# Keys one slot ahead, and the products with the values two slots at a time

## The chip, the cores and the metric

The program runs on one core of a Trainium2 chip. The number that counts is the time of one execution in device microseconds (us), the median of several runs. The core has five engines that work side by side and tell each other of finished work through semaphores: TensorE (PE in the rows: matrix products), VectorE (DVE), ScalarE (ACT), GpSimd (POOL) and the queue that issues the transfers (SP). Each engine takes its own instructions strictly in their order; one that waits holds up all behind it on that engine.

## The reference, cut to what matters

A decoder layer over 32 sequences ("batches") of 112 tokens with 512 features: self-attention, cross-attention to 375 context tokens, a quantised feed-forward layer, each with residuals and layer norms. Only the cross-attention is touched:

```python
q = proj(hs, Wq, bq, S)          # 16 heads of 32
k = proj(at, Wk, bk, T)          # T = 375
v = proj(at, Wv, bv, T)
scores = jnp.einsum('bhsd,bhtd->bhst', q, k) / scale
scores = jnp.clip(scores, -50.0, 50.0)
...
probs = jax.nn.softmax(scores, axis=-1)
ctx = jnp.einsum('bhst,bhtd->bhsd', probs, v)
...
delta = _nan_clean(ctx @ Wo.T + bo)
...
delta = (delta - mu) / jnp.sqrt(var + EPS_LN) * ln_gamma + ln_beta
```

## The kernel before

Three stages follow each other, with a barrier between: `self_attention`, `cross_attention`, `ffn`. In `cross_attention` each batch is worked in four slots h = 0 to 3; a slot holds 4 of the 16 heads. The order on each engine is written out by hand in the `body` functions, and `steps` runs batches 0 and 1, a loop of pairs, and batches 30 and 31.

The work of one batch on TensorE, all products in float32 or as three products of split halves (`PASSES`):
- `keys(b, m)`: 12 matmuls of 376 columns (L874) give the keys of slot m in a bank of PSUM, `bKV`; ScalarE adds the bias and moves them into `kf[:, m, :]` (L730).
- `values(b, t)`: 12 matmuls of 512 columns (L887) for one third t of the context tokens; ScalarE moves them into `v` (L736).
- scores (L942): 24 recorded matmuls that use 32 rows of the array each, four at a time, into the four banks of `bSC`. ScalarE takes the exponentials into `pr[h % 2]` (L751), VectorE clamps and masks them in three pieces (L841), GpSimd adds the three pieces into `psum` (L701, L704).
- `attend(b, h)`: the products of the exponentials with the values (L919), 24 recorded matmuls that use 32 columns of the array each, and `sums(b, h)`: 8 more in the same layout that sum the exponentials over the tokens (L928), both into bank `bPV[h % 2]`.
- VectorE divides (`attended`: L787, L789, L793, L795) and writes the split halves `cT`.
- `output(b)`: 12 matmuls of 512 columns with the output weights (L900). VectorE's `tail1` (L800 to L808), `tail2` (L813 to L825) and `tail3` (L829, L831) finish the batch, with a power on GpSimd between them (`norm` L690, `norm2` L694).

The context of a batch comes in by a transfer into `craw`; ScalarE (`split_high`, L723) and VectorE (`split_low`, L767) split it into `cx`.

What order holds before: in slot h of batch b, TensorE makes scores(b, h), then `attend` and `sums` of the slot before, then in slot 1 `output(b - 1)`, and then the keys of slot h of the NEXT batch and one of its thirds of values. So before the first scores all four slots of keys and all three thirds of values of batch 0 are made, and in batch 31 no keys or values are left. `pr` has two buffers.

## Time and profile before

| | |
|---|---|
| median of 3 runs | 1554.0 us (1553.78 to 1556.58) |
| the profiled execution | 1554.15 us, of which its span (first to last instruction) 1552.3 us |
| self-attention and its set-up | from 0 to about 395 us |
| cross-attention, first matmul | at 400.3 us |
| cross-attention, scores of batch 1 slot 0 / batch 31 slot 0 | at 443.5 us / 1257.9 us |
| feed-forward, first instruction | at 1300.3 us |
| TensorE busy over the span | 94% |
| VectorE, ScalarE, GpSimd busy | 70%, 41%, 37% |
| mean granted TensorE clock, share of full | 0.975 |

In the rows, times are from the start of the span. A matmul's own duration includes time in which the next one already runs; so what a block of matmuls costs is read from its start to the start of the next block. "L874" is line 874 of the kernel before; the new kernel has other line numbers for the same code.

### The profile page before, as it was taken

What the parts mean: (1) busy time and instruction counts of PE and PEld (TensorE: products, weight loads), DVE (VectorE), ACT (ScalarE), POOL (GpSimd) and SP (SyncE); (2) the same over time, 40 slices, a digit from 0 to 9 for tenths busy, and PEclk for the clock granted to TensorE, in tenths of its full rate; (3) what the DMA queues carried; (4) which work ended last, traced back from release to release, by engine and by line L of the source; (5) the groups of instructions that cost most, each with busy time, mean ns of one, the idle gap of its engine ahead of it and who ended that gap; (6) DMA issues with size and microseconds to landing.
All of it is one profiled execution on the core that took longest, in us unless ns stands there. A gap on an engine that the chain in (4) does not pass through costs nothing. (4 is left out here: it accounts for less than half of the span.)

```text
span 1552.3 us, 33463 instructions
## 1 busy us (share of the span) xinstructions
PE 1457.4 (94%) x13281; PEld 1129.5 (73%) x13290; DVE 1080.9 (70%) x2039; ACT 640.8 (41%) x828; POOL 567.0 (37%) x487
## 2 busy tenths in 40 slices
PE   7999999997899999999999999999999974998886
PEld 3688888886788888888888888888888852554332
DVE  3756665653278787777778777777877785775788
ACT  2333333332343333434343343434333322888852
POOL 0000000000045455544545554454555453651453
PEclk9999999998899999999999999999999986999999
DMA  6022222322411112121211212121121103287953
GB/s 210 28 83 92 98 98 98 99 102 63 133 34 59 56 38 75 38 75 38 60 53 38 75 38 75 38 61 52 39 74 38 56 13 92 70 284 268 342 183 109
DMA packets 80405, 138.58 MB, mean 89 GB/s; under 512 B 4882, under 2 KB 52498, under 8 KB 78562
## 3 DMA queue, kind: packets, MB, share of 16 engines
q1 hardware_dynamic: 80354, 137.87, 27.5%
q8 instruction: 35, 0.57, 0.2%
q14 instruction: 16, 0.13, 0.0%
HBM read 93.82 MB, written 44.04 MB: 89 GB/s over the span
## 5 line engine op out<-in xcount | busy, mean ns | idle before, releaser
L874 PE MATMUL xa_bKV<-xa_cx,wA 128*128 128x376 f32 x1536 | 289.6, 338 | 7.4 <-DVE xa_cx L767 7.4
L887 PE MATMUL xa_bKV<-wZ,xa_cx 128*125 128x512 f32 x1152 | 288.7, 399 | 0.0
L874 PEld LDWEIGHTS xa_bKV<-xa_cx,wA 128*128 128x128 f32 x1536 | 266.9, 189 | 22.1 <-issue 13.1
L841 DVE TENSOR_SCALAR xa_pr<-xa_pr,xa_keep 125x448 f32<-125x448 f32 x384 | 151.8, 452 | 162.5 <-ACT xa_pr L751 162.2
L701 POOL TENSOR_TENSOR xa_psum<-xa_pr 125x448 f32<-125x448 f32 x128 | 148.0, 1157 | 296.1 <-DVE xa_pr L841 296.1
L887 PEld LDWEIGHTS xa_bKV<-wZ,xa_cx 128*125 128x125 f32 x1152 | 208.7, 186 | 54.6 <-issue 10.6
L730 ACT ACTIVATE xa_kf<-xa_bKV,xa_bk 128x376 f32<-128x376 f32 x128 | 73.5, 575 | 293.4 <-PE xa_bKV L874 293.3
L751 ACT ACTIVATE xa_pr<-xa_bSC 125x1344 f32<-125x1344 f32 x128 | 165.6, 1293 | 40.4 <-PE xa_bSC L942 40.4
L704 POOL TENSOR_TENSOR xa_psum<-xa_psum,xa_pr 125x448 f32<-125x448 f32 x128 | 149.9, 1171 | 12.3 <-POOL xa_psum L701 4.4
L736 ACT COPY xa_v<-xa_bKV 125x512 f32<-125x512 f32 x96 | 56.3, 587 | 205.8 <-PE xa_bKV L887 205.8
L1311 PE MATMUL ff_bF<-w2q,ff_hq 128*128 128x512 bf16 x439 | 102.7, 392 | 24.0 <-DVE ff_hq L1228 22.1
L942 PEld LDWEIGHTS xa_bSC<-xa_qf,xa_kf 32*125 32x125 f32 x3072 | 95.3, 183 | 36.2 <-issue 36.2
L942 PE MATMUL xa_bSC<-xa_qf,xa_kf 32*125 32x112 f32 x3072 | 118.0, 282 | 1.2 <-ACT xa_pr L751 1.2
L787 DVE RECIPROCAL xa_rinv<-xa_bPV 128x112 f32<-128x112 f32 x128 | 109.0, 851 | 0.0
L795 DVE SCALAR_TENSOR_TENSOR xa_cT<-xa_at,xa_bv,xa_cT 128x112 fp32r<-128x112 f32 x128 | 103.3, 807 | 4.6
L919 PE MATMUL xa_bPV<-xa_pr,xa_v 125*32 125x112 f32 x3072 | 101.3, 265 | 5.2 <-DVE xa_pr L841 4.9
L1311 PEld LDWEIGHTS ff_bF<-w2q,ff_hq 128*128 128x128 bf16 x448 | 44.4, 101 | 82.0 <-issue 32.0
L900 PE MATMUL xa_bKV<-wQ,xa_cT 128*112 128x512 f32 x384 | 99.7, 409 | 3.4 <-DVE xa_cT L795 3.4
L1289 PE MATMUL ff_bF<-ff_xqT,w1q 128*128 128x448 bf16 x512 | 99.3, 355 | 0.5 <-DVE ff_xqT L1198 0.5
L227 POOL TENSOR_TENSOR sa_rstd<-sa_ve,sa_half 112x4 f32<-112x4 f32 x8 | 8.1, 1007 | 235.4 <-DVE sa_ve L356 235.4
L472 PE MATMUL sa_bM<-wZ,sa_xn 128*112 128x512 f32 x384 | 90.7, 395 | 0.0
L694 POOL TENSOR_TENSOR xa_rstd<-xa_ve,xa_half 112x1 f32<-112x1 f32 x32 | 59.7, 1865 | 74.4 <-DVE xa_ve L825 74.4
(170 smaller groups left out, 2208.4 us busy)
## 6 DMA issues: line engine op xcount, KB each, us to landing
wraw<-in_ctxT SPq DMA_DIRECT2D x32, 752.0 KB, 5.5
ff_hr<-h_scratch SPq DMA_DIRECT2D x7, 2048.0 KB, 11.1
wraw<-in_w SPq DMA_DIRECT2D x8, 1024.0 KB, 7.6
sa_raw<-in_x SPq DMA_DIRECT2D x8, 896.0 KB, 5.8
x_scratch<-sa_qraw SPq DMA_DIRECT2D x8, 896.0 KB, 5.0
xa_qf<-q_scratch SPq DMA_DIRECT2D x32, 224.0 KB, 5.4
xa_x<-x_scratch SPq DMA_DIRECT2D x32, 224.0 KB, 5.0
x_scratch<-xa_x SPq DMA_DIRECT2D x32, 224.0 KB, 2.3
```

Source lines behind the costliest of these rows:

```text
L701: nc.gpsimd.tensor_tensor(psum01[:], third(h, 0), third(h, 1), ALU.add).then_inc(p01_ok, 1)
L704: nc.gpsimd.tensor_tensor(psum[h % 2][:], psum01[:], third(h, 2), ALU.add).then_inc(ps_ok, 1)
L751: nc.scalar.activation(pr[h % 2][:], bSC[0:TW, :, 0:TC * S], ACT.Exp, scale=XSCALE).then_inc(exp_ok, 1)
L787: nc.vector.reciprocal(rinv[:], bank[:, S:2 * S]).then_inc(ri_ok, 1)
L795: nc.vector.scalar_tensor_tensor(out=cT[1][:, h, :], in0=at[:], scalar=bvt[:, h:h + 1], in1=cT[0][:, h, :].bitcast(F32), op0=ALU.add, op1= ...
L841: nc.vector.tensor_scalar(third(h, t), third(h, t), EM50, bound, ALU.max, ALU.min).then_inc(pr_ok, 1)
L874: mm = nc.tensor.matmul(bKV[par][:, 0:TP], w["k"][l][:, c, m * P:(m + 1) * P], cx[par][r][:, c, :], start=c == 0 and k == 0, stop=c == C - ...
L887: mm = nc.tensor.matmul(bKV[1 - par][0:TW, 0:D], cx[par][l][:, c, t * TW:(t + 1) * TW], w["v"][r][:, c, :], start=c == 0 and k == 0, stop= ...
L900: mm = nc.tensor.matmul(bKV[1 - par][0:S, 0:D], cT[l][:, c, :], w["o"][r][:, c, :], start=c == 0 and k == 0, stop=c == C - 1 and k == 2)
L919: mm = nc.tensor.matmul(bank[j * HD:(j + 1) * HD, 0:S], v[par][:, t, h * P + j * HD:h * P + (j + 1) * HD], pr[h % 2][:, j, t * S:(t + 1) * ...
L942: mm = nc.tensor.matmul(bSC[0:TW, j, t * S:(t + 1) * S], kf[own, h, t * TW:(t + 1) * TW], qf[par][own, h, :], start=True, stop=True)
L1311: mm = nc.tensor.matmul(bF[(UT * u + j) % 8][:, 0:D], hq[:, u % 2, k * M2 + m, j * P:(j + 1) * P], w2q[:, k * M2 + m, :], start=k == 0 and ...
```

## The change

Four things are changed, all in `cross_attention`:
- Keys are made one slot ahead instead of four: slot h makes the keys of slot h + 1 of the same batch, and slot 3 those of slot 0 of the next. Values: slot 0 makes third 2 of its own batch, slots 2 and 3 make thirds 0 and 1 of the next. `output(b - 1)` stays in slot 1, now without values beside it. Each slot now has one block of keys and one block of 512-column matmuls.
- `attend` and `sums` are made two slots at a time: in slot 2 those of slots 0 and 1, in slot 0 of the next batch those of slots 2 and 3. VectorE's `attended` follows in pairs; `pr` has four buffers.
- Keys always use bank `bKV[0]`, values and output `bKV[1]`.
- On VectorE, `split_low` moves from slot 2 to the head of slot 1 (one batch later), `tail2` from slot 2 to the head of slot 3, ahead of that slot's clamps; on GpSimd `norm2` moves ahead of the sums of slot 3; on ScalarE `split_high` moves from slot 1 to slot 3.

```diff
-        pr = [n.sb(f"pr{i}", [TW, NJ, TC * S]) for i in range(2)]
+        pr = [n.sb(f"pr{i}", [TW, NJ, TC * S]) for i in range(C)]
...
             def body(b, par, pair):
                 for h in range(C):
-
+                    if h == 3 and not first(b):
+                        norm2(b - 1)
                     pool.wait_ge(pr_ok, 12 * b + 3 * h + 3)
...
-            for h in range(C):
-                keys(0, 0, h)
-                if h < TC:
-                    values(0, 0, h)
-                if h == 1:
-                    split_high(1, 1)
+            values(0, 0, 0)
+            keys(0, 0)
+            values(0, 0, 1)
+            split_high(1, 1)
...
-                    wait(act, pv_done, s - 1)
-                    wait(act, ps_ok, s - 1)
-                    nc.scalar.activation(pr[h % 2][:], bSC[0:TW, :, 0:TC * S], ACT.Exp, scale=XSCALE).then_inc(exp_ok, 1)
...
+                    wait(act, pv_done, s - 3)
+                    wait(act, ps_ok, s - 3)
+                    nc.scalar.activation(pr[h][:], bSC[0:TW, :, 0:TC * S], ACT.Exp, scale=XSCALE).then_inc(exp_ok, 1)
+                    if h == 3 and not (isinstance(b, int) and b >= B - 2):
                         split_high(b + 2, par)
+                    if h < C - 1:
+                        keys(b, h + 1)
+                    elif not last(b):
+                        keys(b + 1, 0)
+                    if h == 0:
+                        values(b, par, 2)
+                    elif h >= 2 and not last(b):
+                        values(b + 1, 1 - par, h - 2)
...
             def body(b, par, pair):
                 for h in range(C):
+                    if h == 1 and not last(b):
+                        split_low(b + 1, 1 - par)
+                    if h == 3 and not first(b):
+                        tail2(b - 1, 1 - par)
                     dve.wait_ge(exp_ok, 4 * b + h + 1)
...
-                    if h > 0:
-                        attended(b, h - 1)
-                    elif not first(b):
+                    if h == 0 and not first(b):
+                        attended(b - 1, C - 2)
                         attended(b - 1, C - 1)
...
+                    if h == 2:
+                        attended(b, 0)
+                        attended(b, 1)
...
-                    if h > 0:
-                        attend(b, par, h - 1)
-                        sums(b, h - 1)
-                    elif not first(b):
-                        attend(b - 1, 1 - par, C - 1)
-                        sums(b - 1, C - 1)
-                    if h == 1 and not first(b):
-                        output(b - 1, 1 - par)
-                    if not last(b):
-                        if h >= 2:
-                            values(b + 1, 1 - par, h - 1)
-                        keys(b + 1, 1 - par, h)
-                        if h == 0:
-                            values(b + 1, 1 - par, 0)
+                    if h == 2:
+                        for i in range(2):
+                            attend(b, par, i)
+                            sums(b, i)
+                    elif h == 0 and not first(b):
+                        for i in range(2, C):
+                            attend(b - 1, 1 - par, i)
+                            sums(b - 1, i)
+                    if h < C - 1:
+                        keys(b, par, h + 1)
+                    elif not last(b):
+                        keys(b + 1, 1 - par, 0)
+                    if h == 0:
+                        values(b, par, 2)
+                    elif h == 1:
+                        if not first(b):
+                            output(b - 1)
+                    elif not last(b):
+                        values(b + 1, 1 - par, h - 2)
```

TensorE before the change, in the middle of the loop, slots 3 and 0 of a batch; each row is a first matmul with the semaphores it waits for, or the 11 (or 3) after it:

```order
L942 MATMUL xa_bSC<-xa_qf,xa_kf 125x112 x11
L915 ISA
L919 MATMUL xa_bPV<-xa_pr,xa_v 32x112 [waits xa_cthi_ok,xa_pr_ok]
L919 MATMUL xa_bPV<-xa_pr,xa_v 32x112 x11
L928 MATMUL xa_bPV<-xa_psum,xa_ones 32x112 [waits xa_ps_ok]
L928 MATMUL xa_bPV<-xa_psum,xa_ones 32x112 x3
L882 REGISTER_ALU
L887 MATMUL xa_bKV<-wZ,xa_cx 125x512 [waits xa_v_ok]
L887 MATMUL xa_bKV<-wZ,xa_cx 125x512 x11
```

TensorE after the change, in the middle of the loop, slot 0 and into slot 1:

```order
L906 MATMUL xa_bPV<-xa_pr,xa_v 32x112 [waits xa_cthi_ok,xa_pr_ok]
L906 MATMUL xa_bPV<-xa_pr,xa_v 32x112 x11
L915 MATMUL xa_bPV<-xa_psum,xa_ones 32x112 [waits xa_ps_ok]
L915 MATMUL xa_bPV<-xa_psum,xa_ones 32x112 x3
L902 ISA
L906 MATMUL xa_bPV<-xa_pr,xa_v 32x112 [waits xa_cthi_ok,xa_pr_ok]
L906 MATMUL xa_bPV<-xa_pr,xa_v 32x112 x11
...
L915 MATMUL xa_bPV<-xa_psum,xa_ones 32x112 x3
L867 MATMUL xa_bKV<-xa_cx,wA 128x376 [waits xa_k_ok]
...
L929 MATMUL xa_bSC<-xa_qf,xa_kf 125x112 x11
L867 MATMUL xa_bKV<-xa_cx,wA 128x376 [waits xa_k_ok]
```

The blocks of 32-column matmuls now stand in pairs, and in every second slot the keys follow the scores at once.

VectorE after the change, around slot 3 (the names carry their buffer numbers: `bPV0` and `bPV1` belong to the two slots of a pair, `pr3` to slot 3):

```order
L842 TENSOR_SCALAR xa_pr2<-xa_pr2,xa_keep 125x4x112 x3
L786 RECIPROCAL xa_rinv<-xa_bPV0 128x112
...
L786 RECIPROCAL xa_rinv<-xa_bPV1 128x112
...
L794 SCALAR_TENSOR_TENSOR xa_cT1<-xa_at,xa_bv,xa_cT0 128x112
L812 TENSOR_TENSOR xa_rr<-xa_rstd,xa_rs 112x1
L816 SCALAR_TENSOR_TENSOR xa_x11<-xa_dl,xa_rr,xa_x11 112x512
L819 BN_STATS xa_st<-xa_x11 112x6
L822 BN_AGGR xa_mv<-xa_st 112x2
L824 TENSOR_SCALAR xa_ve2<-xa_mv 112x1
...
L842 TENSOR_SCALAR xa_pr3<-xa_pr3,xa_keep 125x4x112 x3
```

The same place before (the clamps of slot 3 write `pr1`):

```order
L825 TENSOR_SCALAR xa_ve2<-xa_mv 112x1
...
L767 TENSOR_TENSOR xa_cx01<-wraw,xa_cx00 128x1504
...
L841 TENSOR_SCALAR xa_pr1<-xa_pr1,xa_keep 125x4x112 x3
L787 RECIPROCAL xa_rinv<-xa_bPV0 128x112
L789 TENSOR_TENSOR xa_at<-xa_bPV0,xa_rinv 128x112
```

Before slot 3's clamps VectorE now has two `attended` and `tail2` in a row, where it had one `attended`, `tail2` and `split_low`.

## Rows read from the trace of the kernel before

**Rows 1.** Windows: busy time by engine, then granted clock, DMA share, GB/s.

```profile
395.50:405.70 10.20, 5.40 (x16) 5.14 (x17) 3.54 (x7) 2.02 (x2) 0.16 (x2) 0.50 0.70 166
443.50:1257.90 814.40, 814.40 (x9604) 681.08 (x9604) 626.25 (x1229) 312.80 (x359) 405.21 (x330) 1.00 0.17 51
1272.70:1289.80 17.10, 8.52 (x75) 5.68 (x76) 11.77 (x22) 0.00 (x0) 6.74 (x7) 0.50 0.23 67
```

**Rows 2.** Timeline, TensorE, loop: start, busy, line, out<-in, rows*columns, count.

```profile
816.77 0.92 PE L942 MATMUL xa_bSC<-xa_qf,xa_kf 32*125 32x112 f32 x24
817.63 0.78 PE L919 MATMUL xa_bPV<-xa_pr,xa_v 125*32 125x112 f32 x24
...
818.53 3.02 PE L887 MATMUL xa_bKV<-wZ,xa_cx 128*125 128x512 f32 x12
...
825.29 2.34 PE L874 MATMUL xa_bKV<-xa_cx,wA 128*128 128x376 f32 x12
827.47 2.94 PE L887 MATMUL xa_bKV<-wZ,xa_cx 128*125 128x512 f32 x12
830.33 0.92 PE L942 MATMUL xa_bSC<-xa_qf,xa_kf 32*125 32x112 f32 x24
```

**Rows 3.** The same, windows of one nanosecond: later matmuls of the small blocks.

```profile
817.75 0.37 PE L919 MATMUL xa_bPV<-xa_pr,xa_v 125*32 125x112 f32 x8
818.13 0.28 PE L919 MATMUL xa_bPV<-xa_pr,xa_v 125*32 125x112 f32 x4
818.32 0.28 PE L928 MATMUL xa_bPV<-xa_psum,xa_ones 125*32 125x112 f32 x4
```

**Rows 4.** Timeline, TensorE, from the first matmul to batch 1, slot 0.

```profile
400.30 4.10 PE L874 MATMUL xa_bKV<-xa_cx,wA 128*128 128x376 f32 x12 [7.43 <-DVE xa_cx L767]
...
407.67 2.23 PE L874 MATMUL xa_bKV<-xa_cx,wA 128*128 128x376 f32 x12
409.74 2.94 PE L887 MATMUL xa_bKV<-wZ,xa_cx 128*125 128x512 f32 x12
...
419.47 0.92 PE L942 MATMUL xa_bSC<-xa_qf,xa_kf 32*125 32x112 f32 x24
420.32 2.34 PE L874 MATMUL xa_bKV<-xa_cx,wA 128*128 128x376 f32 x12
...
443.48 0.92 PE L942 MATMUL xa_bSC<-xa_qf,xa_kf 32*125 32x112 f32 x24
```

**Rows 5.** Timeline, TensorE, batch 31: scores of slot 0, and output(31).

```profile
1257.88 0.92 PE L942 MATMUL xa_bSC<-xa_qf,xa_kf 32*125 32x112 f32 x24
...
1285.14 5.14 PE L900 MATMUL xa_bKV<-wQ,xa_cT 128*112 128x512 f32 x12 [3.42 <-DVE xa_cT L795]
```

**Rows 6.** Timeline, VectorE, the same batch as Rows 2.

```profile
809.50 0.68 DVE L800 TENSOR_TENSOR xa_dl<-xa_bKV,xa_bo 112x512 f32<-112x512 f32 x1
...
811.42 0.74 DVE L808 SCALAR_TENSOR_TENSOR xa_dl<-xa_dl,xa_mv,xa_gam 112x512 f32<-112x512 f32 x1
...
816.93 0.15 DVE L813 TENSOR_TENSOR xa_rr<-xa_rstd,xa_rs 112x1 f32<-112x1 f32 x1
...
819.07 1.73 DVE L767 TENSOR_TENSOR xa_cx<-wraw,xa_cx 128x1504 fp32r<-128x1504 f32 x1
820.71 1.17 DVE L841 TENSOR_SCALAR xa_pr<-xa_pr,xa_keep 125x448 f32<-125x448 f32 x3
...
824.38 0.53 DVE L829 TENSOR_SCALAR xa_x<-xa_x,xa_mv,xa_rstd 112x512 f32<-112x512 f32 x1
```

**Rows 7.** Timeline, GpSimd, the same batch: the power of norm2, the second sum.

```profile
819.21 2.00 POOL L694 TENSOR_TENSOR xa_rstd<-xa_ve,xa_half 112x1 f32<-112x1 f32 x1 [2.33 <-DVE xa_ve L825]
...
823.19 1.14 POOL L704 TENSOR_TENSOR xa_psum<-xa_psum,xa_pr 125x448 f32<-125x448 f32 x1
```

**Rows 8.** Timeline, ScalarE, the same batch: keys moved, exponentials taken.

```profile
816.88 0.57 ACT L730 ACTIVATE xa_kf<-xa_bKV,xa_bk 128x376 f32<-128x376 f32 x1 [1.47 <-PE xa_bKV L874]
817.76 1.29 ACT L751 ACTIVATE xa_pr<-xa_bSC 125x1344 f32<-125x1344 f32 x1 [0.31 <-PE xa_bSC L942]
```

More of the change, by code:

```diff
@@ L708, in body @@
                         norm(b - 1)
-                    if h == 2 and not first(b):
-                        norm2(b - 1)
             steps(pool, body, B, 2)
@@ L904, in _ @@
             pe.wait_ge(const_ok, 2)
-            for h in range(C):
-                keys(0, 0, h)
-                if h < TC:
-                    values(0, 0, h)
+            values(0, 0, 0)
+            keys(0, 0, 0)
+            values(0, 0, 1)
             def attend(b, par, h):
```

69 lines of the change are left out of this document (24 added, 45 removed).

## The prediction

> **What bounds the kernel now.** First the windows: from 443.50 to 1257.90 us TensorE is busy in all of the 814.40 us, at the full granted clock of 1.00 (2.4 GHz) [rows 1]. No wait ends last in this stage; TensorE's own order of work does. So an edit there is worth what it takes out of TensorE's blocks, start to start, as long as nothing else comes late. One batch takes (1257.88 - 443.48) / 30 = 27.147 us [rows 4, 5].
>
> Next the timeline of one batch. From start to start, scores cost 0.86 us (816.77 to 817.63), attend and sums together 0.90 (817.63 to 818.53), keys 2.18 (825.29 to 827.47) and a 512-column block 2.86 (827.47 to 830.33): 6.80 per slot, 27.2 per batch [rows 2]. The small blocks run in groups of four matmuls. Attend's second group starts at 817.75 and its last at 818.13, four groups later: a pitch of 0.095. But the first group takes 0.12 (817.63 to 817.75), 0.025 more; and from the last group of sums (818.32) to the next full-array block (818.53) it is 0.21, 0.115 more than a pitch [rows 2, 3]. So each stay in the 32-column layout costs 0.14 us beside its work. Where scores are followed by keys with no attend between (only batch 0, slot 0), they cost 0.85, just as before attend [rows 2, 4]: leaving the scores costs the same whatever comes next.
>
> Last, the two ends. The first scores start 19.17 us after the first matmul (400.30 to 419.47) [rows 4], after four blocks of keys and three of values; and in batch 31, without keys and values, TensorE waits much of the time (at the end it is busy 8.52 of 17.10 us [rows 1]): its last output starts 27.26 us after the scores of slot 0 (1257.88 to 1285.14) [rows 5].
>
> **TensorE in the loop: less.** The matmuls are the same. Four stays in the 32-column layout per batch become two, so 2 x 0.14 = 0.28 us less per batch: 26.87. The new slots: an even one is scores 0.86, a pair (8 + 8 groups less shared ends: 0.90 + 8 x 0.095 = 1.66), keys 2.18, values 2.86 = 7.56; an odd one 5.90. From batch 1 to batch 31: 30 x 0.28 = **8.4 us**. The step sums(0) to attend(1), in the same layout but into another bank, is in no row; I count a pitch. Its bounds are nothing extra and the 0.14 of a stay. I take nothing, since attend to sums goes on at the pitch (last group of attend at 818.13, last of sums two groups later at 818.32: 2 x 0.095) though sums has a semaphore wait of its own [rows 3]. By the Trainium skill ("TensorEngine Tiling (Array Packing)", "Key Properties") changing the mode drains the array and changing only the tile does not; that speaks for the lower bound, and no row here has this very step.
>
> **The start: less.** The new kernel needs values, keys, values before the first scores. The clock is 0.50 until 405.7 [rows 1]; a 512-column block at that clock takes 5.14 [rows 5], so the first ends at 405.4, keys (2.07, 407.67 to 409.74, without a layout change ahead [rows 4]) at about 407.7, and values at 410.45 with the entry to scores. Then, with the costs above: keys(1) 411.3, values(2) 413.5, scores(1) 416.3, keys(2) 417.2 to 419.4. Here a wait is new: scores(2) of batch 0 have no 512-column block ahead (there is no output yet), so they wait until ScalarE has moved the keys: start 0.11 after the next block would (816.77 to 816.88), 0.57 long, 0.1 to signal: 0.8 [rows 2, 8]. Scores(2) at 420.2, pair to 422.7, keys(3) 424.9, values 427.7, slot 3 5.9: batch 1 slot 0 at 433.6 instead of 443.48: **9.8 us less**. It is not work removed but three keys blocks, a values block and an attend moved behind this point, 10.2 us, less the wait of 0.8 and the other small ones.
>
> **The end: more.** What was moved comes back in batch 31, now in time that was idle. With t = 0 at scores(31, 0): slot 1 at 7.6, slot 2 at 13.5, its pair and keys(3) to 18.2, wait for the keys moved 0.8, scores(3) 19.0 to 19.8. Then VectorE decides. Its chain starts at output(30), done at 13.5 + 0.2: tail1 809.50 to 811.42 + 0.74 less overlap = 2.6 (16.3); clamps and one attended are 820.71 to 824.38 = 3.67 with clamps 1.17, so an attended is 2.5 and clamps with two are 6.2 (22.5); tail2 816.93 to 819.07 = 2.1 (24.6) [rows 6]. Only now slot 3's clamps: psum of slot 3 is complete 823.19 + 1.14 - 820.71 = 3.6 later [rows 6, 7], at 28.2. Meanwhile VectorE has clamped (25.8) and done tail3 (1.3) and the attended of slot 2 (to 29.6); that of slot 3 ends at 32.1, and output(31) starts: 32.0 against 27.26, **4.7 us more**. Behind it all is as before.
>
> **The sum.** 9.8 + 8.4 - 4.7 = 13.5 us less. The profiled execution took 1554.15, 0.15 over the median of 1554.0. 1554.15 - 13.5 = 1540.65, on the median's scale 1540.5.
>
> **What hides the rest, and what is late next.** In the loop, with t = 0 at scores(b, 0); exponentials end 2.28 after a slot's start (816.77 to 817.76 + 1.29) [rows 2, 8]:
> - Keys one slot ahead: keys done at 0.86 + 2.18 in an odd slot, moved 0.7 later, used after another 2.9 us of values or output: 2.2 us to spare. Without that block it costs 0.8 (counted at both ends).
> - Slot 0, VectorE: clamps 2.3 to 3.5, two attended to 8.5. output(b - 1) asks for them at 7.56 + 0.86 + 2.18 = 10.6: 2.1 to spare. Then split_low 1.73 (10.2) [rows 6] against exponentials at 9.8: clamps of slot 1 end 11.4, psum 13.8, asked for by sums(1) at 13.46 + 0.86 + 0.6 + 0.2 + 0.6 = 15.7. Split_low is needed only at the values of slot 2, 18.2.
> - Slot 3 is the tight one. The chain above gives psum(3) at 28.2; sums(3) stand in slot 0 of the next batch, at 26.87 + 0.86 + 0.6 + 0.2 + 0.6 = 29.1. The added order is norm2 on GpSimd ahead of those sums, queued behind VectorE's tail2. In the row it took 2.00, since it began at 819.21 beside split_low (819.07, 1.73 long) [rows 6, 7]; so alone it is about 2.00 - (820.80 - 819.21) = 0.4. Next to clamps it lies between: 0.4, hidden under 1.2 us of clamps, or 2.00 from 24.7, which puts the sums 0.9 later: psum(3) at 29.1. So 0.9 us to spare, or none. Who waits behind: TensorE in sums(3), and all its keys and values. I take no stall.
> - ScalarE: split_high now follows slot 3's exponentials and delays the keys' move by under 1 us, inside the 2.2 to spare. With four buffers the exponentials wait only for what TensorE and GpSimd did three slots back, long done: nothing. SP: its order is kept; the context's transfer is issued after split_low (t = 10.2) and read in slot 3 (23), 13 us later, where before it had the three slots from the split in slot 2 to slot 1 (20): I count nothing.
>
> On the pair of DVE and GpSimd, what the row shows is that GpSimd's power ended 0.4 after VectorE's large operation did. The Trainium skill ("SBUF — State Buffer", "Who interferes with whom") says that the engine that issues first holds the shared ports for its whole instruction and the other fully blocks. By that rule each of the three clamps, tail3's first operation and the power could stand in one another's way in slot 3, and the sum would lose what the second rival below prices; the same trace agrees on the one pair it has.
>
> **The rivals.**
> - *Pairs give TensorE nothing.* If sums(0) to attend(1) costs the 0.14 (a drain for the other bank, or three semaphore waits in the queue), the loop stays at 27.15 and only the ends remain: 9.8 - 4.7 = 5.1 less, 1549.0. For: no row shows that step. Against: keys to values change banks too and go at 2.07 [rows 4]. Chance 0.10.
> - *Slot 3's psum becomes the bound (slower).* If the power blocks for 2.0 and in turn pushes the clamps by about 1 us more, psum(3) comes at 30.0 instead of 28.2, 0.9 after TensorE asks; that repeats in all 31 batches: +28, 1540.5 + 28 = 1568. It decides from a stall of 13.5 / 31 = 0.44 us per batch, psum(3) at 29.5. For: VectorE has two attended, tail2 and the clamps in a row now. Against: my 2.5 per attended is one that ran against GpSimd's second sum, and the second of a pair has no such neighbour. Chance 0.06; a milder stall, 0.05 to 0.3 us per batch, 1542 to 1550: 0.08.
> - *The clock at the end.* It fell to 0.50 at 1272.70, 14.8 us after scores(31, 0), in a stretch where TensorE waited often [rows 1, 5]. Now TensorE is full until 19.8, then all but idle for 9 us. If output(31) at 32 still runs at 2.4 GHz, it takes about 3 instead of 5.14: 1538.4. It is in the forecast's own range.
> - *Something at the ends I don't see* (the two new keys waits longer, the context of batch 1 late in the shorter start): up to 4 us more. Chance 0.06, mostly still faster.
>
> **How the numbers follow.** Forecast: 1540.5, chance 0.70, own range 1537.5 to 1543.5 (clock at the end -2.1, its recovery in the feed-forward +-1, an attended shorter by 0.8 in the last chain -1). To leave out no more than 0.2 the range goes down to 1537 and up to 1549, the first rival and most mild stalls. A measurement here can tell 0.2%, 3.1 us, from no change. Faster (under 1550.9): 0.70 + 0.10 + most of 0.08 and 0.06 = 0.90. Slower (over 1557.1): 0.06. The same: 0.04.
>
> **What would show it.** Right: batch to batch 26.87 on TensorE, no wait of sums for psum in the loop; sums(0) to attend(1) in 0.19 (two pitches); scores of batch 1 slot 0 at 433.6; output(31) 32 after scores(31, 0). Wrong: a batch of 27.15 (no gain from pairs), or TensorE idle before sums with GpSimd's second sum as the releaser, once per batch in slot 0; or a first scores block later than 410.5.

## The result and the profile after

The changed kernel takes 1541.2 us, median of five runs (1539.58 to 1541.61), against 1554.0 for the kernel before on the same chip (1553.78 to 1557.89, five runs): ratio 0.991, 95% interval 0.9896 to 0.9923. So 12.8 us are gone, where 13.5 were forecast. The page of the changed kernel begins:

```profile
span 1539.4 us, 33524 instructions
```

The span is cut at five places that both kernels have. Each number is a difference of two starts in the TensorE timeline of one profiled execution, but for "output(31) to its addition", which ends at VectorE's first operation on that product.

| stretch, us | before | after | difference | forecast |
|---|---|---|---|---|
| start of the span to the first matmul of the stage | 400.30 | 401.86 | +1.6 | 0 |
| first matmul to scores(1, 0) | 43.18 | 33.47 | -9.7 | -9.8 |
| scores(1, 0) to scores(31, 0), 30 batches | 814.40 | 807.40 | -7.0 | -8.4 |
| scores(31, 0) to output(31) | 27.26 | 30.94 | +3.7 | +4.7 |
| output(31) to its addition | 5.18 | 4.92 | -0.3 | 0 |
| on to the first matmul of the feed-forward | 11.12 | 11.12 | 0 | 0 |
| feed-forward | 250.89 | 249.72 | -1.2 | 0 |
| span | 1552.3 | 1539.4 | -12.9 | -13.5 |

The first row is scatter: the code before it is the same in all 13 profiled executions of this study, and the first matmul starts between 399.98 and 403.50. The feed-forward takes 248.1 to 251.3 in them, which covers the -1.2 too; but the kernel before, keys_only and the three pairs kernels have 249.6 to 251.3 and the other eight 248.1 to 250.1, so these runs don't exclude that a part of it comes from the end.

**The start.** TensorE of the changed kernel, from the first matmul to batch 1, slot 0 (start, busy, line, output <- operands, rows*columns, count, and idle time before it with what ended it); it answers to [rows 4]:

```profile
401.86 5.46 PE L878 MATMUL xa_bKV<-wZ,xa_cx 128*125 128x512 f32 x12 [7.42 <-DVE xa_cx L766]
...
412.15 0.92 PE L929 MATMUL xa_bSC<-xa_qf,xa_kf 32*125 32x112 f32 x24
...
421.87 0.92 PE L929 MATMUL xa_bSC<-xa_qf,xa_kf 32*125 32x112 f32 x24 [0.66 <-ACT xa_kf L729]
...
435.33 0.92 PE L929 MATMUL xa_bSC<-xa_qf,xa_kf 32*125 32x112 f32 x24
```

The first scores come 10.29 after the first matmul (forecast 10.15), the new wait for the moved keys is there, at scores(0, 2), with 0.66 of idle time; from start to start keys and wait take 2.99 (418.88 to 421.87) instead of 2.17, so the wait costs 0.82 (forecast 0.8). Batch 1 starts at 33.47 (forecast 33.3). How closely this fits is in part chance: the eight profiled kernels with this order of blocks give 32.3 to 33.5, and the granted clock comes back at different points of the first blocks in them (pool_plus1, with 32.3, has 0.64 instead of 0.50 from 400 to 405 us, and its first block takes 4.39 instead of 5.46).

**The loop.** The same engine at the end of one batch and the start of the next, where [rows 2] showed one slot of before. Slot 0 begins at 812.12; the groups behind its scores are attend(2), sums(2), attend(3), sums(3) of the batch before:

```profile
812.12 0.92 PE L929 MATMUL xa_bSC<-xa_qf,xa_kf 32*125 32x112 f32 x24
812.97 0.78 PE L906 MATMUL xa_bPV<-xa_pr,xa_v 125*32 125x112 f32 x24
813.57 0.38 PE L915 MATMUL xa_bPV<-xa_psum,xa_ones 125*32 125x112 f32 x8
813.76 0.76 PE L906 MATMUL xa_bPV<-xa_pr,xa_v 125*32 125x112 f32 x24
814.34 0.38 PE L915 MATMUL xa_bPV<-xa_psum,xa_ones 125*32 125x112 f32 x8
814.64 2.33 PE L867 MATMUL xa_bKV<-xa_cx,wA 128*128 128x376 f32 x12
816.81 2.92 PE L878 MATMUL xa_bKV<-wZ,xa_cx 128*125 128x512 f32 x12
819.67 0.92 PE L929 MATMUL xa_bSC<-xa_qf,xa_kf 32*125 32x112 f32 x24
...
825.57 0.92 PE L929 MATMUL xa_bSC<-xa_qf,xa_kf 32*125 32x112 f32 x24
```

No row here has idle time before it. From sums(2) to attend(3), the step that no row of before showed, it is 813.57 to 813.76: 0.19, two groups at the pitch of 0.095, so changing the bank costs nothing that these rows show. The even slot takes 7.55 (forecast 7.56) and the odd one 5.90.

**Slot 3, the tight one.** VectorE and GpSimd in the slot ahead of that, which answer to [rows 6, 7]:

```profile
809.25 1.18 DVE L842 TENSOR_SCALAR xa_pr<-xa_pr,xa_keep 125x448 f32<-125x448 f32 x3
```

```profile
809.37 0.74 POOL L694 TENSOR_TENSOR xa_rstd<-xa_ve,xa_half 112x1 f32<-112x1 f32 x1 [4.09 <-DVE xa_ve L824]
810.51 1.39 POOL L702 TENSOR_TENSOR xa_psum<-xa_pr 125x448 f32<-125x448 f32 x1 [0.40 <-DVE xa_pr L842]
811.97 1.14 POOL L705 TENSOR_TENSOR xa_psum<-xa_psum,xa_pr 125x448 f32<-125x448 f32 x1
```

The power of norm2 takes 0.74, next to the clamps, and is done before them: the clamps keep their length (1.18) and the first sum waits for them and not for the power. The second sum ends at 811.97 + 1.14 = 813.11 and sums(3) ask for it at 814.34: 1.2 us to spare.

**The end.** TensorE in batch 31, in place of [rows 5]:

```profile
1242.73 0.92 PE L929 MATMUL xa_bSC<-xa_qf,xa_kf 32*125 32x112 f32 x24
...
1261.69 0.92 PE L929 MATMUL xa_bSC<-xa_qf,xa_kf 32*125 32x112 f32 x24 [0.66 <-ACT xa_kf L729]
...
1267.91 1.35 PE L906 MATMUL xa_bPV<-xa_pr,xa_v 125*32 125x112 f32 x24 [4.39 <-DVE xa_pr L842]
1270.56 0.60 PE L915 MATMUL xa_bPV<-xa_psum,xa_ones 125*32 125x112 f32 x8 [1.30 <-POOL xa_psum L705]
1273.67 4.88 PE L888 MATMUL xa_bKV<-wQ,xa_cT 128*112 128x512 f32 x12 [2.51 <-DVE xa_cT L794]
```

Scores(31, 3) come 18.96 after scores(31, 0), as forecast (19.0), and output(31) 30.94 (forecast 32.0), after waits for the clamps, the sum and VectorE's chain. It takes 4.88, at half the clock, by the window (its columns are those of [rows 1]):

```profile
1267.50:1277.70 10.20, 5.97 (x42) 4.06 (x43) 5.87 (x11) 0.00 (x0) 3.75 (x4) 0.50 0.38 112
```

### The profile page after: what moved, and what is told of

Read it like the earlier page. It is cut to its first block and busy times, and to the rows that moved or that the text cites. A ratio compares the mean times of both kernels' runs of the same rounds, so it can differ in the third digit from the quotient of the medians.

```text
span 1539.4 us, 33524 instructions
## 1 busy us (share of the span) xinstructions
PE 1449.4 (94%) x13290; PEld 1128.2 (73%) x13290; DVE 1058.9 (69%) x2039; ACT 640.3 (42%) x828; POOL 567.1 (37%) x487
## 5 line engine op out<-in xcount | busy, mean ns | idle before, releaser
L867 PE MATMUL xa_bKV<-xa_cx,wA 128*128 128x376 f32 x1536 | 298.6, 343 | 0.0
L878 PE MATMUL xa_bKV<-wZ,xa_cx 128*125 128x512 f32 x1152 | 284.4, 396 | 7.4 <-DVE xa_cx L766 7.4
L867 PEld LDWEIGHTS xa_bKV<-xa_cx,wA 128*128 128x128 f32 x1536 | 258.4, 188 | 17.9 <-issue 10.8
L878 PEld LDWEIGHTS xa_bKV<-wZ,xa_cx 128*125 128x125 f32 x1152 | 213.6, 187 | 51.9 <-issue 7.8
L702 POOL TENSOR_TENSOR xa_psum<-xa_pr 125x448 f32<-125x448 f32 x128 | 156.0, 1219 | 242.2 <-DVE xa_pr L842 242.2
L1304 PEld LDWEIGHTS ff_bF<-w2q,ff_hq 128*128 128x128 bf16 x448 | 44.1, 100 | 81.3 <-issue 30.5
L794 DVE SCALAR_TENSOR_TENSOR xa_cT<-xa_at,xa_bv,xa_cT 128x112 fp32r<-128x112 f32 x128 | 96.3, 753 | 4.5
L888 PE MATMUL xa_bKV<-wQ,xa_cT 128*112 128x512 f32 x384 | 96.3, 400 | 2.5 <-DVE xa_cT L794 2.5
L690 POOL TENSOR_TENSOR xa_rstd<-xa_ve,xa_half 112x1 f32<-112x1 f32 x32 | 64.2, 2008 | 71.3 <-DVE xa_ve L806 71.3
```

Source lines behind the costliest of these rows:

```text
L702: nc.gpsimd.tensor_tensor(psum01[:], third(h, 0), third(h, 1), ALU.add).then_inc(p01_ok, 1)
L794: nc.vector.scalar_tensor_tensor(out=cT[1][:, h, :], in0=at[:], scalar=bvt[:, h:h + 1], in1=cT[0][:, h, :].bitcast(F32), op0=ALU.add, op1= ...
L867: mm = nc.tensor.matmul(bKV[0][:, 0:TP], w["k"][l][:, c, m * P:(m + 1) * P], cx[par][r][:, c, :], start=c == 0 and k == 0, stop=c == C - 1 ...
L878: mm = nc.tensor.matmul(bKV[1][0:TW, 0:D], cx[par][l][:, c, t * TW:(t + 1) * TW], w["v"][r][:, c, :], start=c == 0 and k == 0, stop=c == C ...
L1304: mm = nc.tensor.matmul(bF[(UT * u + j) % 8][:, 0:D], hq[:, u % 2, k * M2 + m, j * P:(j + 1) * P], w2q[:, k * M2 + m, :], start=k == 0 and ...
```

## The experiments

Eleven kernels ran. "Before" is the kernel before in the same series, on the same chip. The loop is given per batch, from scores(1, 0) to scores(31, 0) over 30; start and end are the second and fourth stretch of the table above.

| kernel | median us (lowest to highest, runs) | before | ratio, 95% | start | loop | end |
|---|---|---|---|---|---|---|
| before | | | | 43.2 | 27.147 | 27.3 |
| after_again | 1540.7 (1538.2 to 1542.2, 5) | 1553.9 | 0.9919, 0.9905 to 0.9932 | 33.2 | 26.913 | 30.9 |
| keys_only | 1553.5 (1552.2 to 1556.6, 11) | 1553.9 | 0.9997, 0.9988 to 1.0006 | 35.6 | 27.245 | 30.6 |
| pairs_only | 1569.9 (1569.5 to 1570.6, 4) | 1553.9 | 1.0107, 1.0092 to 1.0123 | 42.4 | 27.586 | 30.5 |
| end_first | 1538.6 (1536.7 to 1541.9, 5) | 1553.9 | 0.9911, 0.9896 to 0.9926 | 33.5 | 26.913 | 28.1 |
| pool_plus1 | 1542.5 (1540.9 to 1543.8, 4) | 1553.4 | 0.9932, 0.9915 to 0.9949 | 32.3 | 26.960 | 31.6 |
| pool_plus2 | 1579.0 (1578.1 to 1580.4, 4) | 1553.4 | 1.0165, 1.0148 to 1.0182 | 33.2 | 28.125 | 34.0 |
| pairs_mended | 1564.0 (1562.1 to 1566.2, 5) | 1555.0 | 1.0057, 1.0043 to 1.0071 | 42.1 | 27.345 | 30.6 |
| warm_gaps | 1537.1 (1536.2 to 1537.7, 4) | 1555.0 | 0.9885, 0.9870 to 0.9900 | 33.5 | 26.913 | 27.9 |
| warm_all | 1536.5 (1535.8 to 1539.9, 4) | 1555.0 | 0.9888, 0.9872 to 0.9903 | 33.5 | 26.913 | 27.9 |
| pairs_slot1 | 1549.9 (1547.1 to 1552.4, 8) | 1554.3 | 0.9970, 0.9960 to 0.9981 | 43.4 | 26.887 | 29.9 |
| best | 1536.3 (1534.2 to 1537.2, 4) | 1554.3 | 0.9888, 0.9873 to 0.9903 | 33.2 | 26.913 | 27.9 |

The theory at the outset was that of the prediction: two stays fewer in the 32-column layout make the loop shorter, the keys one slot ahead make the start shorter, and the end gives a part back. Its rivals were that the keys do the work in the loop too, and that slot 3 is closer to a stall than the timeline says.

### The change once more

No edit; it gives the scatter for the others.

> The changed kernel once more, beside the next three on one chip, so that differences of 2 to 7 us can be told. Both theories: 1541.2 us, within 1 us; a batch in the loop takes 26.91 us on TensorE again. If the 1.6 us that the profiled execution lost in the first 50 us of the untouched self-attention was chance, this profile shows another number there.

Measured: 1540.7, and the same 807.40 over the 30 batches, 26.913 each. The first matmul starts at 400.83 instead of 401.86. The loop repeats within 0.01 us; the stretches outside it scatter.

### The keys alone

The new order of keys and values, with attend, sums and attended of one slot at a time, as before the change:

```diff
 # TensorE, in the changed kernel
-                    if h == 2:
-                        for i in range(2):
-                            attend(b, par, i)
-                            sums(b, i)
-                    elif h == 0 and not first(b):
-                        for i in range(2, C):
-                            attend(b - 1, 1 - par, i)
-                            sums(b - 1, i)
+                    if h > 0:
+                        attend(b, par, h - 1)
+                        sums(b, h - 1)
+                    elif not first(b):
+                        attend(b - 1, 1 - par, C - 1)
+                        sums(b - 1, C - 1)
```

VectorE's attended go singly in the same way.

> Half of the change: keys one slot ahead as in the changed kernel, but attend and sums of one slot at a time, in every slot (and VectorE's attended one at a time). Theory (each stay in the 32-column layout costs TensorE 0.12 us beside its work, measured as half of 27.147 - 26.913): four stays per batch again, so a batch of 27.15 us, 7.0 us more over 30 batches; at the end VectorE has one attended less (1.9 us) between the last clamps of slot 2 and those of slot 3. So 1541.2 + 7.0 - 1.9 = 1546.3. Rival (the loop became shorter because the keys moved, and pairs give nothing): batch 26.91, 1539.3.

Measured: 1553.5, no difference from before. That is a miss by 7 us. The three stretches tell where it went. The start is 35.6, not some 34: in batch 0 TensorE waits for GpSimd's sum, and one attend more than in the changed kernel stands ahead of batch 1. TensorE of this kernel:

```profile
422.07 0.40 PE L912 MATMUL xa_bPV<-xa_psum,xa_ones 125*32 125x112 f32 x8 [0.93 <-POOL xa_psum L705]
...
800.88 0.78 PE L903 MATMUL xa_bPV<-xa_pr,xa_v 125*32 125x112 f32 x24
```

The loop is 27.245, so 0.098 per batch or 2.9 us longer than before. The step from scores to attend is 0.92 in slot 1 (799.96 to 800.88) and 0.85 in slot 2 (806.82 to 807.67). In slot 1, attend needs values that ScalarE has only just moved, since values of third 2 now stand one block ahead of that slot:

```profile
800.07 0.58 ACT L735 COPY xa_v<-xa_bKV 125x512 f32<-125x512 f32 x1 [2.19 <-PE xa_bKV L875]
```

That move ends at 800.65 and attend starts at 800.88. The step accounts for 0.07; that the move causes it is likely but not shown. The trace names no releaser for it, and in batch 30, outside the loop of pairs, the move stands at the same place (1236.04, 0.10 after the scores) and the step is 0.85. The rest, 0.03, is what the new key order costs in the changed kernel too (below). Then the end is 3.4 longer. So the keys bring 7.6 at the start and lose 2.9 + 3.4 elsewhere: alone they are worth next to nothing, and in the changed kernel, whose pairs take the values one slot later, the 0.07 is gone.

### The pairs alone

The kernel before, with four buffers of exponentials and pairs on TensorE and VectorE; everything else as it was:

```diff
 # TensorE, in the kernel before; VectorE's attended likewise
-                    if h > 0:
-                        attend(b, par, h - 1)
-                        sums(b, h - 1)
-                    elif not first(b):
-                        attend(b - 1, 1 - par, C - 1)
-                        sums(b - 1, C - 1)
+                    if h == 2:
+                        for i in range(2):
+                            attend(b, par, i)
+                            sums(b, i)
+                    elif h == 0 and not first(b):
+                        for i in range(2, C):
+                            attend(b - 1, 1 - par, i)
+                            sums(b - 1, i)
```

> The other half: keys four slots ahead as before the change, but attend, sums and attended two slots at a time with four buffers; tail2 and split_low stay in slot 2. Theory: two stays per batch, 26.91 us, 7.0 us less than the kernel before, the start as before (first scores 19.2 us after the first matmul), the end 1 to 2 us longer by the second attended: 1554.0 - 7.0 + 1.5 = 1548.5. But two places are tight: output(b-1) now asks for the attended pair at 8.4 us after scores(b,0), and the pair is done at 8.3 in the changed kernel; and split_low ahead of slot 3's clamps brings the psum of slot 3 at about 28.9, asked for at 29.1. Rival (the pairs need the new order of keys and of split_low): TensorE waits in one of these places each batch, 0.3 to 0.7 us, 9 to 20 us in all, and the time is 1557 to 1568.

Measured: 1569.9, 1.1% slower, as the expectation's rival had it and 21 us over its theory. It is the late sum of slot 3 that the prediction's slower rival feared, in another version of the kernel and from another cause. TensorE waits once per batch, in sums(3):

```profile
802.86 0.76 PE L922 MATMUL xa_bPV<-xa_pr,xa_v 125*32 125x112 f32 x24
804.13 0.40 PE L931 MATMUL xa_bPV<-xa_psum,xa_ones 125*32 125x112 f32 x8 [0.51 <-POOL xa_psum L704]
```

Start to start it is 1.27 instead of the 0.58 of the changed kernel: 0.69 lost. 27.586 - 0.69 = 26.90, so without the wait the pairs alone would have given the whole of the loop's gain. VectorE shows why the sum is late:

```profile
826.20 1.73 DVE L767 TENSOR_TENSOR xa_cx<-wraw,xa_cx 128x1504 fp32r<-128x1504 f32 x1
827.85 1.17 DVE L841 TENSOR_SCALAR xa_pr<-xa_pr,xa_keep 125x448 f32<-125x448 f32 x3
```

In slot 2 it now does the clamps, two attended, tail2 and then split_low, and only behind that slot 3's clamps. The changed kernel has moved split_low to slot 1. That looked like a side matter in the diff; the next two runs show that the pairs gain nothing without it.

### The pairs with split_low behind slot 3

pairs_only, with tail2 and norm2 in slot 3 as in the change, and split_low at the end of that slot:

```diff
 # VectorE and GpSimd, in pairs_only
+                    if h == 3 and not first(b):   # tail2 on VectorE, norm2 on GpSimd,
+                        ...                       # at the head of slot 3
-                        if h == 2:
+                        if h == 3:
                             split_low(b + 2, par)
```

> pairs_only (keys four slots ahead, attends in pairs) with VectorE's and GpSimd's order of the changed kernel in slot 3: tail2 at the head of slot 3, norm2 ahead of its sums, and split_low behind slot 3's clamps instead of ahead of them. Theory (pairs_only lost 0.7 us per batch in sums(3), because split_low's 1.7 us stood ahead of slot 3's clamps, and nothing else): a batch of 26.91 us on TensorE, 20 us less than pairs_only over 30 batches, 1549.7; what then stays to the changed kernel, 8 to 9 us, is the start (42.4 against 33.5 us to batch 1) and the last batch. Rival (pairs need the keys one slot ahead for another reason): a batch over 27.1, over 1556.

Measured: 1564.0. A miss by 14 us: the clamps are early enough now, and TensorE still waits. From attend(3) to sums(3) it is 1.03 instead of 0.58, so 0.45 are lost per batch:

```profile
829.75 0.76 PE L921 MATMUL xa_bPV<-xa_pr,xa_v 125*32 125x112 f32 x24
830.78 0.40 PE L930 MATMUL xa_bPV<-xa_psum,xa_ones 125*32 125x112 f32 x8 [0.27 <-POOL xa_psum L705]
```

VectorE and GpSimd of this kernel show the cause:

```profile
827.85 1.87 DVE L766 TENSOR_TENSOR xa_cx<-wraw,xa_cx 128x1504 fp32r<-128x1504 f32 x1
```

```profile
828.22 2.50 POOL L705 TENSOR_TENSOR xa_psum<-xa_psum,xa_pr 125x448 f32<-125x448 f32 x1
```

GpSimd's second sum takes 2.50 instead of 1.14, and ends 1.0 after split_low (829.72) does. It begins 0.37 into split_low. So it lost 1.36 of the 1.50 us in which both ran. The Trainium skill ("SBUF — State Buffer", "Who interferes with whom") says that a VectorE instruction with two inputs in SBUF contends with a GpSimd instruction that reads SBUF, and that the shared ports are an exclusive lock. By that rule the sum would wait until 829.72 and then take its 1.14, to 830.86; it ended at 830.72, so this row agrees within 0.15 us. The same VectorE operation had stood in [rows 6, 7], with the power as the victim.

### The pairs with split_low in slot 1

pairs_mended, with the split of the context one slot earlier on ScalarE than in the kernel before (slot 0, where the change has it in slot 3), and on VectorE at the head of slot 1, as in the change:

```diff
-                    if h == 1 and not (isinstance(b, int) and b >= B - 2):
+                    if h == 0 and not (isinstance(b, int) and b >= B - 2):
                         split_high(b + 2, par)
 # VectorE: split_low(b + 2, par) at the head of slot 1 and no longer in slot 3
```

> pairs_mended with the split of the context one step earlier: split_high in slot 0, split_low at the head of slot 1, where GpSimd is idle (the place that the changed kernel has). Theory (what pairs_mended still lost, 0.43 us per batch, is GpSimd's second sum of slot 3, 2.50 us instead of 1.15, because split_low of 1.87 us ran beside it): a batch of 26.9 to 27.0 us, the second sum of slot 3 back at 1.15, 13 us less than pairs_mended, 1551. Rival (with keys four slots ahead another wait takes its place): a batch over 27.2, 1560 or more.

Measured: 1549.9, and 26.887 per batch without any wait. The second sum of slot 3 is back at its own length, 1.14; then TensorE of this kernel in an odd slot:

```profile
822.15 1.14 POOL L705 TENSOR_TENSOR xa_psum<-xa_psum,xa_pr 125x448 f32<-125x448 f32 x1
```

```profile
830.38 0.92 PE L943 MATMUL xa_bSC<-xa_qf,xa_kf 32*125 32x112 f32 x24
831.23 3.03 PE L901 MATMUL xa_bKV<-wQ,xa_cT 128*112 128x512 f32 x12
834.10 2.22 PE L875 MATMUL xa_bKV<-xa_cx,wA 128*128 128x376 f32 x12
836.25 0.92 PE L943 MATMUL xa_bSC<-xa_qf,xa_kf 32*125 32x112 f32 x24
```

This kernel gives three sizes. First, a stay in the 32-column layout costs (27.147 - 26.887) / 2 = 0.13, not 0.14. Second, the new key order gives the loop nothing and takes 0.026 per batch, the difference to the 26.913 of the changed kernel: the odd slot with the output is 5.87 here, and 5.90 there, where the 512-column block stands between keys and scores. The banks of keys and values differ between the two kernels as well, and no run tells the order from the banks. Third, the keys one slot ahead are worth what the ends give: the start goes from 43.4 to 33.5, the end from 29.9 to 30.9. By the medians the changed kernel is 12.8 under its before and this one 4.4, so the keys are worth 8.4 on top of the pairs with their mended slots; keys_only showed them as worth nothing alone. Whether moving split_low alone would have been enough for the pairs wasn't run: tail2 and norm2 stand in slot 3 in this kernel too.

### How far slot 3 is from a stall

One and two sums more on GpSimd in slot 3, ahead of the sums proper, into a tile that nobody reads:

```diff
 # GpSimd, in the changed kernel; range(1) in pool_plus1, range(2) in pool_plus2
+                    if h == 3:
+                        for k in range(1):
+                            nc.gpsimd.tensor_tensor(dum[:], third(h, 0), third(h, 1), ALU.add).then_inc(dum_ok, 1)
+                            pool.wait_ge(dum_ok, 1 * b + k + 1)
```

> The changed kernel with one more addition of two thirds (1.16 us, result unused) on GpSimd ahead of the sums of slot 3 in every batch: about 1.24 us later there. In the changed kernel's trace psum of slot 3 is complete at 813.1 and sums(3) start at 814.3, 1.2 us to spare. Theory (that spare time is real and nothing else hangs on it): 0 to 0.2 us of wait per batch, 0 to 6 us in all, 1541 to 1547. Rival (GpSimd's order in slot 3 is already on the path, hidden by overlap in the rows): 1.2 us per batch, 1580.

> The same with two more additions, about 2.5 us later. Theory: 2.5 - 1.2 = 1.3 us of wait in sums(3) per batch, 30 x 1.3 = 38 us, 1580, with GpSimd's second sum as the releaser. Rival (already on the path): 75 us, 1617. Third (the wait is swallowed, because other work has more room than the rows show): under 1550.

Measured: 1542.5 with one, 1579.0 with two. With one, GpSimd and then TensorE in slot 3 and the next slot 0:

```profile
811.39 1.15 POOL L710 TENSOR_TENSOR xa_psum<-xa_psum,xa_pr 125x448 f32<-125x448 f32 x1
```

```profile
812.59 0.40 PE L920 MATMUL xa_bPV<-xa_psum,xa_ones 125*32 125x112 f32 x8
```

The sum ends at 812.54 and is used at 812.59: the slack is used up, and the batch is 0.05 longer. With two, the waits of TensorE from 440 to 1235 us, 28 batches (engine, tile, line <- what it waits for: us, times, longest):

```profile
PE xa_bPV L920 <- POOL xa_psum L710: 29.1, 28, 1.1
```

The batch grows by 28.125 - 26.913 = 1.21. A sum and its signal take 1.21 (810.18 to 811.39 in pool_plus1): 2 x 1.21 - 1.23 of slack = 1.19. So the slack read from the profile, 1.23, is the real one, and the 1.19 of delay beyond it cost 1.21 per batch. The rival of a psum bound therefore decides from 1.2 us of delay. A power of 2.00, 0.9 later at the sums by the prediction's working, would still have found room; with the clamps pushed by 1 us as well, as the rival had it, it would not.

### The end, in another order

In batch 31 the two attended that output(31) waits for go ahead of tail2 and tail3 of batch 30:

```diff
-                    if h == 3 and not first(b):
+                    if h == 3 and not first(b) and not last(b):
                         tail2(b - 1, 1 - par)      # tail3, and norm2 on GpSimd, likewise
 ...
             attended(B - 1, C - 2)
             attended(B - 1, C - 1)
+            tail2(B - 2, 0)
+            tail3(B - 2, 0)
             tail1(B - 1)
```

> The changed kernel with another order in the last batch alone: VectorE clamps slot 3 before tail2 of batch 30, and tail2, norm2 and tail3 of batch 30 come after the last attended, beside output(31) on TensorE, where VectorE is idle for 4.9 us. Theory (the end is VectorE's chain, 2.1 us of tail2 and 0.7 to 1.2 us of tail3 stand in it): output(31) starts 28 us after scores(31,0) instead of 30.9, time 2.8 us less, 1538.4. Rival (TensorE's low clock or a wait of its own sets the end): within 0.5 us of the changed kernel.

Measured: 1538.6. Output(31) starts 28.1 after scores(31, 0), still at half the clock (4.63):

```profile
1269.47 4.63 PE L891 MATMUL xa_bKV<-wQ,xa_cT 128*112 128x512 f32 x12 [1.97 <-DVE xa_cT L795]
```

Most of the end's loss is VectorE's order: 2.9 of the 3.7 us come back in the profile, and 2.1 in the medians of one series, whose ranges overlap. The other 0.8 isn't taken apart.

### The clock at the end

end_first, with matmuls that nobody reads in the gaps of batch 31, into the scores' bank, from operands that lie there:

```diff
+            def fill(n):
+                for k in range(n):
+                    nc.tensor.matmul(bSC[:, 0, 0:TP], w["k"][0][:, 0, 0:P], cx[1][0][:, 0, :], start=True, stop=True)
+
 # fill(8), fill(9) and fill(11) around attend(31, 3) and sums(31, 3);
 # warm_all: also fill(44) after output(31)
```

> end_first with 8, 9 and 11 matmuls of 376 columns, result unused, in TensorE's three waits after the scores of batch 31 slot 3 (1.4, 1.6 and 1.9 us at full clock, a little shorter than the waits they stand in). Theory (the granted clock fell to half because TensorE waited there, and output(31) pays for it with 4.6 to 4.9 us instead of 2.9): the clock stays at 1.00 through output(31), which takes 2.9 to 3.0; 1.8 us less than end_first, 1536.8. Rival (the clock falls all the same, or the fillers delay attend and sums by their own length at half clock): same as end_first or up to 3 us more.

> warm_gaps with 44 more such matmuls (7.6 us at full clock) behind output(31), in the 11.1 us in which TensorE waits for the last norm, the transfer and the barrier. Theory: as warm_gaps, and the feed-forward's first matmuls, 17 us at half clock until now, start at the full one: 1 to 2 us less again, 1535.3. Rival (the clock falls again in the 4 us of waits behind the barrier, or falls the same whatever is done): as warm_gaps.

Measured: 1537.1 and 1536.5. In the gaps the clock holds. The window of warm_gaps, TensorE busy 11.92 of 17.30 us, and its output:

```profile
1260.00:1277.30 17.30, 11.92 (x132) 9.13 (x130) 15.31 (x31) 1.86 (x2) 6.53 (x8) 1.00 0.08 18
```

```profile
1270.21 3.03 PE L891 MATMUL xa_bKV<-wQ,xa_cT 128*112 128x512 f32 x12
```

Output(31) takes 3.03 instead of 4.63, and yet the addition behind it starts 4.84 after it, as in end_first. VectorE and GpSimd tell why:

```profile
1272.93 1.48 DVE L829 TENSOR_SCALAR xa_x<-xa_x,xa_mv,xa_rstd 112x512 f32<-112x512 f32 x1 [0.67 <-POOL xa_rstd L694]
...
1275.05 0.68 DVE L800 TENSOR_TENSOR xa_dl<-xa_bKV,xa_bo 112x512 f32<-112x512 f32 x1
```

```profile
1272.86 1.27 POOL L686 TENSOR_TENSOR xa_x<-xa_x,xa_bet 112x512 f32<-112x512 f32 x1
```

The 1.6 us that TensorE gained lie under batch 30's tail, whose normalisation takes 1.48 (0.53 in [rows 6], where GpSimd has nothing of that size beside it). The two kernels' medians come from different series (1538.6 and 1537.1; before 1553.9 and 1555.0), so I don't read a gain of the clock from them; the profile shows none, though 1537.1 lies close to the expected 1536.8. In end_first too the normalisation takes 1.49, beside the same addition. In warm_all the clock still falls, only later:

```profile
1270.00:1283.30 13.30, 9.99 (x55) 9.11 (x53) 9.00 (x18) 0.00 (x0) 3.35 (x4) 1.00 0.37 104
1283.30:1293.60 10.30, 3.72 (x22) 2.33 (x23) 6.53 (x22) 0.00 (x0) 1.10 (x8) 0.50 0.74 168
```

The feed-forward takes 249.5 here and 249.3 in warm_gaps: nothing gained. But its first matmuls still run at 0.50, from 1285.46 on, so the expectation's theory was not met, and what they would gain at the full clock stays open.

### The end reordered once more

warm_gaps, with GpSimd's x1_beta(31) ahead of norm2(30), so that it runs beside nothing of VectorE's tail3, and with batch 30's largest absolute value taken behind the addition of output(31):

```diff
+            x1_beta(B - 1, 1)
             norm2(B - 2)
-            x1_beta(B - 1, 1)
 # VectorE: tail3(30) is cut in two, its TENSOR_REDUCE follows tail1(31)
```

> warm_gaps with GpSimd's x1_beta(31) ahead of norm2(30), and VectorE's last reduction for batch 30 behind tail1 of batch 31. Theory (in warm_gaps output(31) takes 3.0 us, but VectorE starts on it only 4.8 us after its start, because tail2 and tail3 of batch 30 stand ahead, one of their operations 1.5 us beside x1_beta): VectorE starts 3.3 to 3.6 us after output(31) starts, 1.0 us less to the feed-forward, 1536.0. Rival (the order of the ends doesn't matter, something else sets it): 4.8 us again, 1537.

Measured: 1536.3, 1.1% under the kernel before. That is the lowest median, but the medians can't tell it from the two before it: against its own before it is 18.0 lower, warm_gaps 17.9 and warm_all 18.5. The profile tells more. VectorE's last two steps before and at the addition:

```profile
1271.55 0.55 DVE L865 TENSOR_SCALAR xa_x<-xa_x,xa_mv,xa_rstd 112x512 f32<-112x512 f32 x1 [0.67 <-POOL xa_rstd L694]
1272.01 0.68 DVE L805 TENSOR_TENSOR xa_dl<-xa_bKV,xa_bo 112x512 f32<-112x512 f32 x1
```

The normalisation is down from 1.48 to 0.55, and the addition starts 3.19 after output(31) instead of 4.84: in the profile the clock's gain now counts, and the feed-forward starts 14.55 after output(31) instead of 15.98. A version with all four slots' products in one stay (another 0.13 per batch or so) wasn't tried: attend and sums have two banks, TensorE would write one of them while VectorE reads it, and PSUM's other six banks are taken.

## Why the prediction was right

**What bounds the loop: right.** TensorE's own blocks set the time, no wait came up, and pairs_slot1 against the kernel before shows that the gain is that of the two stays fewer. The pitch between banks was the choice with the rival "pairs give nothing" behind it, and at 0.19 it is exactly the lower bound. The Trainium skill ("TensorEngine Tiling (Array Packing)", "Key Properties") says that changing the mode, and not just the tile, drains the array; the row agrees, as the mode stays the same there and no time is lost.

**The size of the loop's term: 7.0 instead of 8.4.** The step that was mis-sized is "each stay costs 0.14" and, with it, "a batch of 26.87". A stay costs 0.13 (pairs_slot1), which takes 0.02 per batch, and the new order of keys, with its banks, costs 0.026 that I had counted at nothing by saying that the matmuls are the same: together 0.046 x 30 = 1.4 us. The prediction's own slots, 7.56 and 5.90, add up to 26.92 per batch, which is what came; it took 0.28 from the measured 27.147 instead, though its blocks of before add up to 27.20. The 0.14 was put together from single nanosecond rows, 0.025 and 0.115, each with an error of a hundredth; over 60 stays that hundredth is 0.6 us.

**The start: right, -9.7 for -9.8.** The order of blocks, their costs and the new wait (0.82) are as worked out, but for the first block (5.26 to the next start, for 5.14). The fit to 0.1 is luck, since the start of this order scatters by 1.1 between executions. keys_only and pairs_slot1 show that this term needs both: the blocks moved behind the point come from the keys' order, and one attend of them from the pairs.

**The end: +3.7 instead of +4.7.** TensorE's part was right to 0.1. The term that was mis-sized is "an attended is 2.5". In VectorE's chain two attended are 2.86 + 1.76 = 4.62, not 5.0, and in the last chain they are 2.83 (1268.95 to 1271.78) and 1.84 (1271.78 to 1273.62), not twice 2.5. The first pair in the changed kernel (VectorE, the first operation of each attended, and what follows the pair):

```profile
1259.96 0.85 DVE L786 RECIPROCAL xa_rinv<-xa_bPV 128x112 f32<-128x112 f32 x1
...
1262.82 0.84 DVE L786 RECIPROCAL xa_rinv<-xa_bPV 128x112 f32<-128x112 f32 x1
...
1264.58 0.15 DVE L812 TENSOR_TENSOR xa_rr<-xa_rstd,xa_rs 112x1 f32<-112x1 f32 x1
```

The prediction named this as a reason that the stall was unlikely ("the second of a pair has no such neighbour") and put it at 0.8 in the forecast's own range, but the sum used 2.5 throughout. The price had been read from one attended beside GpSimd's second sum and then used for one that is alone.

**Slot 3: right that it doesn't stall, wrong on the margin.** It said 0.9 to spare or none; it is 1.2, since the sum is complete 27.9 after scores(b, 0) and not 28.2 (the shorter attended), and is asked for at 29.1, as forecast. The power next to the clamps is 0.74 long, near the lower bound of 0.4 and not the 2.00 of [rows 7]. So the choice between the bounds came out right, but the working gave no reason for it, and the same kernel has the other bound too. In slot 1 GpSimd takes the power of norm, of the same form, beside a VectorE operation of 0.74 and the same three clamps (VectorE, then GpSimd):

```profile
827.59 0.74 DVE L807 SCALAR_TENSOR_TENSOR xa_dl<-xa_dl,xa_mv,xa_gam 112x512 f32<-112x512 f32 x1
828.25 1.17 DVE L842 TENSOR_SCALAR xa_pr<-xa_pr,xa_keep 125x448 f32<-125x448 f32 x3
```

```profile
827.76 2.08 POOL L690 TENSOR_TENSOR xa_rstd<-xa_ve,xa_half 112x1 f32<-112x1 f32 x1 [2.00 <-DVE xa_ve L806]
```

That power takes 2.08 and ends 0.42 after the last clamp (829.42); over 30 batches its mean is 2.04, where that of slot 3 has 0.73. No VectorE instruction beside it is longer than 0.85, so the length of the single instruction beside it can't be the whole reason, and what lets the power through in slot 3 stays open; there the prediction was lucky. In slot 1 the long power hurts nobody: the sums behind it end at 832.18 and are asked for some 8 us later.

A late sum of slot 3 does cost what the rival said, though not through the power: pairs_only lost 0.7 per batch because split_low stood ahead of the clamps, and pairs_mended 0.45 because it ran beside the sum. What was missed is that the change's gain hangs on moving split_low, which the prediction only followed through the queue ("needed only at the values of slot 2").

**The clock at the end: didn't come.** Output(31) ran at half the clock, as the sum had it. With fillers it runs at full clock, but the 2.1 us that the rival counted were not there to be had until the tail of batch 30 was out of the way.

The two misses, +1.4 in the loop and -1.0 at the end, nearly cancel in the sum; that 1541.2 came so close to 1540.5 is luck, as the terms were less close. The measured end also moved by -0.3 in output(31)'s own time, and the untouched stretches by +1.6 and -1.2, which the runs here don't explain.

## What to carry to other kernels

When one engine is busy without a gap, count its changes of layout and group what needs the same layout; but first look where the engines that feed the group have their long operations, because grouping makes their results due in bursts: the same pairing made this kernel 1.1% slower with one VectorE operation of 1.7 us in slot 2 and 0.3% faster with it in slot 1 and two shorter steps moved to slot 3. A part of a change that is worth nothing alone can be worth some 8 us on top of another, so test both "this part alone" and "all but this part". And read the price of a short operation from a row with the same neighbours as the place where it will run; where rows give two prices, as for the power here, keep both as bounds.
